# PE's branch over the maximum pass moved ahead of two waits and announced by a prefetch hint; a mask product in 17 pieces; the first layer norm spread over four steps

## What is computed

```python
x = x + tanh(g_xattn[0]) * L0_xattn(_layernorm(x), ctx, ctx, ...)   # 16 heads, softmax over 6404 keys
x = x + tanh(g_ffn[0])   * L0_ffn(_layernorm(x), ...)               # tree-routed leaves, then attention in blocks of 256
x = x + tanh(g_xattn[1]) * L1_xattn(_layernorm(x), ctx, ...)        # the keys are the context and x itself, causal
x = x + tanh(g_ffn[1])   * L1_ffn(_layernorm(x), ...)               # 14 routed experts (top 2) and 2 shared, silu
x = x + tanh(g_xattn[2]) * L2_xattn(ctx, _layernorm(x), ...)        # linear attention, no softmax
x = x + tanh(g_ffn[2])   * L2_ffn(_layernorm(x), ...)               # 8 experts, silu(x Wg) * (x Wu)
x = x + tanh(g_xattn[3]) * L3_xattn(ctx, ctx, _layernorm(x), mask, ...)
x = x + tanh(g_ffn[3])   * L3_ffn(_layernorm(x), ...)               # 8 experts, top 2, capacity 64, gelu
```

## Time and profile before

| | |
|---|---|
| median of 3 runs | 3182.16 us (3170.7 to 3186.71) |
| the profiled execution | 3188.49 us, of which 3186.8 us from the first to the last instruction |
| PE busy | 3054.7 us (96%) |
| ACT busy | 2548.4 us (80%) |
| DVE busy | 443.4 us (14%) |
| POOL busy | 191.9 us (6%) |
| mean granted clock of TensorE | 0.975 of full |

### The profile page before, as it was taken

One profiled execution on the slowest core, in us unless ns is written; L12 is line 12 of the kernel. 1 busy time (PEld: TensorE's weight loads), 2 busy tenths in 40 slices (PEclk: granted clock), 3 DMA queues, 4 the chain that ended last, 5 costly groups with the idle time before them and its releaser, 6 DMA issues.

```text
span 3186.8 us, 56663 instructions
## 1 busy us (share of the span) xinstructions
PE 3054.7 (96%) x18432; PEld 1136.2 (36%) x18432; DVE 443.4 (14%) x1302; ACT 2548.4 (80%) x2960; POOL 191.9 (6%) x699
## 2 busy tenths in 40 slices
PE   6799999999989979999999999899899999999999
PEld 3432222322233532322332323566522222322256
DVE  3510000100012420000120001644300000100012
ACT  3389999999962259999999998332289999999963
POOL 2000000000000000000000000100000000000000
PEclk9989999999989979999999999999989999999999
DMA  7801111111140011111111113110001111111110
GB/s 190 227 33 37 37 37 37 37 38 37 37 110 0 1 29 37 38 38 37 52 50 38 39 36 94 36 55 1 1 31 37 36 37 40 60 38 36 37 39 7
DMA packets 147563, 146.34 MB, mean 46 GB/s; under 512 B 17512, under 2 KB 100956, under 8 KB 147436
## 3 DMA queue, kind: packets, MB, share of 16 engines
q1 hardware_dynamic: 141552, 142.57, 14.4%
q10 hardware_dynamic: 5884, 2.08, 0.3%
HBM read 115.21 MB, written 29.57 MB: 45 GB/s over the span
## 4 chain that ended last, share of the span: by engine, by line
PE 92%; DVE 4%; issue 2%; ACT 1%; DMA 1%; POOL 1%; DVEq 0%; ACTq 0%; SPq 0%; POOLq 0%
PE PS L2095 39%; PE PS L2114 32%; PE PS L717 5%; PE PS L702 5%; PE PS L704 2%; PE PS L1013 2%; PE PS L999 1%; PE PS L1938 1%; PE PS L1948 1%; PE PS L1000 0%; PE PS L1048 0%; PE PS L2075 0%; PE PS L2081 0%; PE PS L2014 0%; PE PS L1034 0%
## 5 line engine op out<-in xcount | busy, mean ns | idle before, releaser
L1874 ACT ACTIVATE probs<-PS 128x1024 f32<-128x1024 f32 x2496 | 2276.9, 1413 | 46.3 <-PE PS L2114 42.6
L2095 PE MATMUL PS<-probs,vr 128*32 128x512 f32 (+1 forms) x9984 | 1333.7, 607 | 1.9 <-DVE accs L2334 1.9
L2114 PE MATMUL PS<-qs,kr 35*128 35x512 f32 (+2 forms) x4992 | 1113.7, 495 | 17.3 <-issue 15.7
L2114 PEld LDWEIGHTS PS<-qs,kr 35*128 35x128 f32 x4992 | 461.9, 185 | 1293.6 <-ACT probs L1874 1103.4
L740 ACT ACTIVATE probs<-PS 128x512 f32<-128x512 f32 x192 | 114.6, 598 | 272.0 <-PE PS L702 143.9
L1708 POOL COPY vr<-vs 128x72 f32 (+1 forms) x624 | 157.9, 254 | 2828.8 <-PE PS L2095 2480.7
L2095 PEld LDWEIGHTS PS<-probs,vr 128*32 128x32 f32 x9984 | 197.7, 108 | 324.8 <-issue 214.3
L2334 DVE COPY accs<-PS 128x512 f32<-128x512 f32 x12 | 8.3, 692 | 1315.2 <-PE PS L2081 1315.2
L717 PEld LDWEIGHTS PS<-wide,probs 128*128 128x128 f32 x1280 | 151.5, 194 | 17.5 <-issue 16.7
L717 PE MATMUL PS<-wide,probs 128*128 128x128 f32 x1280 | 153.8, 277 | 0.5 <-DVE kf L775 0.5
L2332 DVE TENSOR_TENSOR PS<-PS,stair 128x256 f32<-128x256 f32 x64 | 25.3, 430 | 666.5 <-PE PS L2114 666.5
(11 more groups left out here) (299 smaller groups left out, 1158.9 us busy)
## 6 DMA issues: line engine op xcount, KB each, us to landing
kr<-key_pieces SPq DMA_DIRECT2D x1248, 64.0 KB
key_pieces<-kparts SPq DMA_DIRECT2D x36, 288.0 KB, 4.6
kr<-mask_strips SPq DMA_DIRECT2D x624, 4.0 KB
key_pieces<-probs SPq DMA_DIRECT2D x32, 288.0 KB, 4.7
vs<-values SPq DMA_DIRECT2D x2, 3672.0 KB, 16.6
values<-v_next SPq DMA_DIRECT2D x9, 432.0 KB, 5.3
values<-probs SPq DMA_DIRECT2D x8, 432.0 KB, 5.2
accs<-in_ctx SPq DMA_DIRECT2D x12, 192.0 KB, 4.3
```

Source lines behind the costliest of these rows:

```text
L1874: sc.activation(prob[n % RING][:, :, q0:], PS[:, bank:bank + 2, q0:], ACT.Exp, scale=SCALE).then_inc(p_ready, 1)
L2095: last = te.matmul(PS[32 * j:32 * j + 32, 7, q0:], vr[s.buf(c)][:, at_v:at_v + 32], prob[(n + j // 2) % RING][:, j % 2, q0:], start=fresh, ...
L2114: last = te.matmul(o, kr[b][own, p, :], qs[own, T8 // 2 * s.hh + p, 512 * s.qh + q0:512 * s.qh + 512], start=True, stop=True)
```

## The change

In four places:

- PE: `pe.If` is written out as a branch. A hint is placed at the top of the loop over attentions and tied to that branch, so that the branch's target can be fetched ahead. The branch needs the flag alone; the waits for `qc_act` and `qc_dve` stand at the head of each of its two targets.
- POOL: the mask product is 17 instructions of 3 chunks each; the last raises `v_final`.
- DVE: the first norm is cut in parts. Before step 13 come `bn_stats` and `bn_aggr` of the first half, before step 14 those of the second half and one reciprocal root for all eight tiles, before steps 15 and 16 the four `tensor_scalar` of one half each.
- PE: in `project_pe` the bias product stands ahead of the wait for ACT's copy in the second half.

```diff
@@ -333,7 +333,7 @@
                 chain(v.tensor_tensor(tmp, tmp, src, ALU.mult))
                 chain(v.scalar_tensor_tensor(dst, tmp, 1.5, dst, ALU.add, ALU.mult))
 
-        def norm(chain, src, dst, h):
+        def moments(chain, src, h):
 
             v = nc.vector
             for n in range(NH * h, NH * h + NH):
@@ -342,11 +342,32 @@
             for n in range(NH * h, NH * h + NH):
                 last = v.bn_aggr(ln_mv[:, n, :], ln_st[:, n, :])
             chain(last)
-            chain(v.tensor_scalar(ln_ve[:, half(h)], ln_mv[:, half(h), 1], LN_EPS, None, ALU.add))
-            rsqrt(chain, ln_rs[:, half(h)], ln_ve[:, half(h)], ln_sd[:, half(h)])
+
+        def scales(chain, s):
+
+            chain(nc.vector.tensor_scalar(ln_ve[:, s], ln_mv[:, s, 1], LN_EPS, None, ALU.add))
+            rsqrt(chain, ln_rs[:, s], ln_ve[:, s], ln_sd[:, s])
+
+        def centre(src, dst, h):
+
             for n in range(NH * h, NH * h + NH):
-                last = v.tensor_scalar(dst[:, n, :], src[:, n, :], ln_mv[:, n, 0:1], ln_rs[:, n:n + 1], ALU.subtract, ALU.mult)
+                last = nc.vector.tensor_scalar(dst[:, n, :], src[:, n, :], ln_mv[:, n, 0:1], ln_rs[:, n:n + 1], ALU.subtract, ALU.mult)
             return last
+
+        def norm(chain, src, dst, h):
+
+            moments(chain, src, h)
+            scales(chain, half(h))
+            return centre(src, dst, h)
+
+        def first_norm(chain, part):
+
+            if part < 2:
+                moments(chain, x, part)
+            if part == 1:
+                scales(chain, slice(0, NT))
+            if part >= 2:
+                centre(x, xn, part - 2).then_inc(ln_xn, 1)
 
         def ln_dve(chain, k, h):
 
@@ -416,12 +437,12 @@
 
         def project_pe(pe, a, h, bank):
 
+            te = nc.tensor
+            if h == 0:
+                pe.wait_ge(early_ev, EARLY_AT[a] + 1)
+            te.matmul(PS[:, bank, :], ones_row[0:1, :], bo[0:1, a, :].unsqueeze(1).to_broadcast([1, NH, D]), start=True, stop=False, skip_group_check=True)
             if h:
                 pe.wait_ge(atT_ready, a + 1)
-            else:
-                pe.wait_ge(early_ev, EARLY_AT[a] + 1)
-            te = nc.tensor
-            te.matmul(PS[:, bank, :], ones_row[0:1, :], bo[0:1, a, :].unsqueeze(1).to_broadcast([1, NH, D]), start=True, stop=False, skip_group_check=True)
             for j in range(NH):
                 last = te.matmul(PS[:, bank, j * P:j * P + P], att_T[:, (NH * h + j) * P:(NH * h + j + 1) * P], wo[:, a, :], start=False, stop=True, skip_group_check=True)
             last.then_inc(y_ps, 1)
@@ -649,7 +670,9 @@
                 pool.wait_ge(gram_sb, 1)
                 pool.wait_ge(v_in, 32)
                 flat = vs[:, 0:NC, :, :].rearrange("p c h v -> p c (h v)")
-                nc.gpsimd.tensor_tensor(flat, flat, mask_T[:, 0:NC].unsqueeze(2).to_broadcast([P, NC, H * VC]), ALU.mult).then_inc(v_final, 1)
+                for c in range(0, NC, TC):
+                    last = nc.gpsimd.tensor_tensor(flat[:, c:c + TC, :], flat[:, c:c + TC, :], mask_T[:, c:c + TC].unsqueeze(2).to_broadcast([P, TC, H * VC]), ALU.mult)
+                last.then_inc(v_final, 1)
 
 
         def bank_of(m, r, c):
@@ -1979,6 +2002,7 @@
             pe.wait_ge(v_ev, NTILE * TC)
 
             for a in range(3):
+                ahead = pe.mark_branch_hint_location()
                 if a < 2:
                     for h in range(2):
                         ln_pe(pe, 2 * a, h, h)
@@ -2030,11 +2054,13 @@
                         if u == 5:
                             pe.wait_ge(bound_ready, 3)
                             te.transpose(PS[0:1, 7, 0:H], bound[64:64 + H, 0:1], ident[64:64 + H, 64:64 + H]).then_inc(bound_ps, 1)
-                pe.wait_ge(qc_act, QU // 2 * (a + 1))
-                pe.wait_ge(qc_dve, QU // 2 * (a + 1))
                 pe.wait_ge(flag_ready, a + 1)
                 need_max = pe.value_load(flag[0:1, a:a + 1], min_val=0, max_val=1)
-                with pe.If(need_max > 0):
+                pe.br_lt(need_max, 1, on_true=f"first_sweep_{a}", on_false=f"maximum_{a}").branch_hint(ahead)
+                with nc.body(f"maximum_{a}", valid_engines=[mybir.EngineType.PE]):
+                    pe.wait_ge(qc_act, QU // 2 * (a + 1))
+                    pe.wait_ge(qc_dve, QU // 2 * (a + 1))
+
                     def max_scores(c, hh, q0, first=False, xc=None):
                         pe.wait_ge(mx_in[a], KEYS_IN * c + (KEYS_IN * (q0 // 4) + KEYS_IN))
                         for r in range(4):
@@ -2062,7 +2088,10 @@
                     pe.wait_ge(mx_run[a], 8 * (NC + nx) - 8)
                     te.transpose(PS[:, 0, 0:P], run_max[:, :, :].rearrange("p h n -> p (h n)"), ident[:, :]).then_inc(mx_tp[a], 1)
                     pe.wait_ge(mx_out[a], MAX_OUT)
-                pe.end_ifs()
+                    pe.br(f"first_sweep_{a}")
+                nc.switch_bb(f"first_sweep_{a}")
+                pe.wait_ge(qc_act, QU // 2 * (a + 1))
+                pe.wait_ge(qc_dve, QU // 2 * (a + 1))
 
                 def left_scores(s):
 
@@ -2197,11 +2226,11 @@
             with dve.Fori(0, ROUNDS) as j:
                 for off in range(1, UNROLL + 1):
                     k_step(j, off)
-            for i in TAIL:
+            for k, i in enumerate(TAIL):
+                if k == 0:
+                    dve.wait_ge(x_in, 16)
+                first_norm(chain, k)
                 if i == TAIL[-1]:
-                    dve.wait_ge(x_in, 16)
-                    for h in range(2):
-                        ln_dve(chain, 0, h)
                     dve.wait_ge(w_late, WEIGHTS_LATE)
                     for a in range(3):
                         last = v.tensor_copy(edt(wq[:, a, :]), by_head(wq_in[:, a, :]))
```

## The result

| | median us | runs | ratio to before |
|---|---|---|---|
| before | 3180.53 | 6, 3170.7 to 3186.71 | |
| after | 3157.22 | 6, 3149.01 to 3158.84 | 0.9918 [0.9904, 0.9933] |

The change takes 23.3 us off the median. The forecast was 3144.8 from that profile, the range 3126 to 3169.

The account below looks back on a forecast made before the run. PE was taken to bound the kernel (92% of the chain), with gains only where it stands still. 13.0 + 17.0 + 3.7 + 8.6 + 1.4 = 43.7 us off the profiled 3188.49 gave 3144.8, range 3126 to 3169.

Parts of the forecast that it names:

- The branch, its own time: PE's three gaps before the first scores after each branch shrink from 5.2 to 0.9 us each: 13.0 us (bounds 5, 13).
- The clock after it: TensorE's clock stays at full in the sweeps behind the three branches, removing ACT's idle time: 17.0 us, lower bound 0.
- The mask product: DVE's norm beside POOL's pieces ends 9.5 us earlier, small operations lose 5.8 again: 3.7 us (bounds 1.5, 11.5).
- The first norm: End of preparation: step 16's values come 7.1 us earlier, and 1.5 from the clock staying up: 8.6 us (6.9 to 10.3).
- The bias product: After the first attention, it begins earlier, ahead of the wait for ACT's copy: 1.4 us (0.7 to 2.1).
- The clock falls all the same: Rival: the clock drops in the thin first microseconds of the sweeps; gain only 26.7 us, 3161.8; chance 0.28.
- The hint buys nothing: Rival: at the branches only the moved waits gain, 5.2 us, and the clock still falls; total 18.9, 3169.6; chance 0.15.
- The pieces let everything through: Rival: DVE's small operations are not held by POOL's mask pieces; 7.8 us more gain, 3137.0; chance 0.10.
- slower by a straddling loop: Rival: PE's new code layout makes a sweep loop's back edge fetch, 45 us per loop; 3235 from the second; chance 0.04.

Follow-up runs that it names:

- the fill kernel: After, plus matmuls with unused results, two ahead of each score group in the first two chunks of each attention's first sweep: 3146.68 us, ratio 0.9900.
- mask only: The kernel before with only POOL's mask product cut into 17 pieces: 3174.13 us, ratio 0.9994.
- the norm alone: The kernel before with only the first norm spread over the last four preparation steps: 3169.31 us, ratio 0.9973.

## Why the prediction was right or wrong

The sign and the range were right, and the reading of the change's places. The sum, 43.7 us, was twice too large: the range was wide enough to hold a time in which its largest term was nothing. By the stages, means over the four traces that have the old part, against the two of after:

- **The branch, its own time: 13.0, measured 4.4 + 4.2 + 3.8 = 12.4.** Right: branch of 3.43 to 0.36, gap to 0.9; of the 12.4, the kernel without the hint gives 5.3 to the moved waits and 7.1 to the hint. Two details differ. The branch costs 0.36, not the 0.2 of a back edge, hidden beside the query copy. And of the two blocks of q8 only one comes after the hint (between 150.5 and 156); the other is still fetched at 163.8 to 165, without PE standing still.
- **The clock after it: 17.0, measured about nothing.** This step failed: "with a gap of 0.9 us in place of 5.2 I expect it to stay". The old sweeps average 41.4, 32.0 and 40.5 us, those of after 45.8, 33.3 and 35.4. The third wins 5.1; the second loses 1.2 (its six traces with the hint and no fill lie between 30.76 and 33.96), the first loses 4.4: the whole of what its branch had won. Over all six such traces the three sweeps together average 113.1 us, over the four with the old branch 114.0. In the old traces of the first two attentions the clock was back after 10 to 14 us in six of eight cases, and in these it fell 1.6 to 2.7 us before the first scores, so that 8 to 11 us of it lay in the sweep; now it falls 2.4 us into the first sweep and all 20.5 us lie in it. The lower bound of the text, 0, was the better value, and its reason ("PE is held back by ACT") the mechanism. The size of the term was right for the one trace it was read from: the fill kernel, whose clock stays at full, has 105.4 us for the three sweeps, 16.5 less than that trace. But two of its three slow stretches were longer than in most executions; against the mean of the four old traces a full clock is worth 8.5 us, and the change got none of it.
- **The mask product: 3.7, measured 1.6** (67.02 to 65.44). Near the lower bound, 1.5; over all six traces with these pieces it is 2.3. The four `tensor_scalar` behave as worked out where they meet the pieces (3.54 us for 3.8, mask only), but in one old trace of four they were what POOL held; in the other three it was L831's product. The sentence that failed is "I let five pieces pass [...] and eight fall in front of one small operation each": every small operation of the second norm took one piece until POOL was through, all twelve of them in after. The rule of the Trainium skill, SBUF — State Buffer, "Who interferes with whom", was put at 1.5, and the trace agrees with it: each operation is held for the full length of a piece, 0.87 of 0.90 us, and 0.38 of 0.42 with shorter ones. Gated sums, whose first input is in PSUM, pass freely (1.12 for four, beside the pieces as without).
- **The first norm: 8.6, measured 6.9** over all fourteen traces. Its lower end. The stall went nearly as worked out: DVE's values come at 142.94 for 142.0, 6.45 us earlier for 7.1, because step 14 ends 0.95 us late (its values at 129.06 for 128.11), where 0.25 was allowed. The clock did stay up longer, to 150.1, and was then at half for 3.4 us across the query products (3.50 us), where before has 13.7 us; of the 1.5 us booked for it the stage shows some 0.4.
- **The bias product: 1.4, measured 0.6 to 1.0.** The stretch that begins at the transposes ahead of it is 46.7 us in after and 47.79 in before where both have 30.7 us at half clock, 45.4 for 46.0 where both have 27.3 (without the hint and with the fill, against the norm alone). The lower end again: the 0.69 us of lateness. No run has this part alone, so this is argued from two pairs of traces.

Sum: 12.4 - 0.5 + 1.6 + 6.9 + 0.8 = 21.2 us, and the medians differ by 21.3 (3178.27 and 3157.01, same chip) to 23.3.

**The rivals.** *The clock falls all the same*, chance 0.28, is what happened; its 26.7 us, taken from the median of 3182 and not from the profiled 3188.5, give 3155.5, and 3157.2 came; the 26.7 are still 3.4 to 5.4 us more than was measured, in the other terms. *The hint buys nothing* is refuted by the kernel without it, whose branch stages are 7.1 us longer; they are 5.3 us shorter than with the old branch, the 5.2 that the rival gave the moved waits. In the whole time the hint is worth less, 4.7 us by the stages, since the sweeps give some back. Refuted too is the use that I made of the rule of the Trainium skill, Runtime: NRT & Kernel Launch, "Instruction fetch mechanics": without a hint the taken branch stalls, as the rule says (3.33 us), but with a hint ahead of it it does not (0.36). *The pieces let everything through* and *slower by a straddling loop* did not occur. Four of five terms came out at their lower end or below, and what the sum had above it was a part that no row carried.

What stays open: why the clock is back after 3.4 to 6.8 us in the third attention and after 13.7 to 20.5 in the first, in the same kernels, at a gap of 1.13 and 0.89 us.

## What to carry to other kernels

A wait of "issue" in front of a branch that takes 3.4 us is a code fetch, and a hint ahead of enough work removes it. Don't book the clock with it: look at what PE does in the first microseconds behind the gap, and if another engine holds it back there, fill it, or the clock falls anyway. When a long POOL instruction is in DVE's way, cutting it into a row of pieces leaves most of the price unless the pieces are short (13.6 us uncut, 11.7 with 17, 4.8 with 51); better give them out to steps in which DVE has slack (9.5 us net). Before the stretches of one profile are priced, look at a second profile of the same kernel.

## What the runs showed of the hardware

- The compare-and-branch over the maximum pass takes 3.3 to 3.9 us (18 executions in six traces without a hint), with a hint 14.7 to 35.5 us ahead 0.35 to 0.39 (24 executions in eight traces), though at the first branch one of its two blocks is fetched only there.
- TensorE's clock fell from 2.4 to 1.2 GHz within an idle time of 3.8 us, and after one of 0.9 us when the work behind it was thin (1.48 us busy of 2.40). Dense work behind 0.9 us kept it; dense work behind 3.7 to 4.4 us did not: it was down for 20.5, 13.7 and 13.7 us.
- Unused matmuls cost little at full clock where PE has slack (the third sweep takes 35.34 us with them, 34.96 in two kernels without them and with 3.4 us at half clock) and 0.8 us a pair at half clock: the same fill gains 10.5 us with the hint and loses 11 (by the ratios) to 13 (by the medians) without it.
- POOL waits for DVE as DVE does for POOL: a piece of 0.90 us took 2.96 beside DVE's product. A DVE operation of 128x4 takes 0.17 alone, 0.35 beside pieces of 0.42, 0.83 beside pieces of 0.90.
